# A four-layer AdaLN and FFN kernel on one core: small tiles and first-layer weights get other addresses in on-chip memory

## The reference

```python
# L0: 64x64 channel mix per sample, weights mixed by softmax(mlp(cond)); then top-1 routed LoRA (8 experts, rank 16)
out = einsum('boi,bih->boh', agg_w, x) + agg_b[:, :, None]
# L1, L2: grouped 9-tap convolution over the 1024 positions, plus a context vector per channel
out = conv(x, weight, groups=4) + ctx[:, :, None]
# L1 ffn: int8-style row-wise quantised product of 1024x1024
# L2 ffn: 1024x1024 base product + top-2 of 16 experts, rank 64
# L3: channel mix as L0; then up (1024x2048), relu^2, down (2048x1024), a latent path of 512
#     scaled by the two largest gate logits, and a layer norm with gamma, beta and LN_EPS
```

## Time and profile before

| | us |
|---|---|
| median of 3 runs | 1837.11 |
| lowest, highest | 1836.74, 1840.3 |
| the profiled execution's own time | 1837.11 |
| its span, first to last instruction | 1835.3 |
| PE busy | 1717.5 (94%) |
| DVE, ACT, POOL busy | 823.1, 459.5, 339.9 |

### The profile page before, as it was taken

The page is one execution under the profiler, slowest core; times in us unless marked ns, Lnnn a source line. Parts: engine busy times, 40 slices in busy tenths (PEclk is TensorE's granted clock), DMA queues, the critical chain, the costliest instruction groups (busy, mean ns, idle before and its releaser), DMA issues.

```text
span 1835.3 us, 22240 instructions
## 1 busy us (share of the span) xinstructions
PE 1717.5 (94%) x8396; PEld 1409.7 (77%) x8396; DVE 823.1 (45%) x1453; ACT 459.5 (25%) x694; POOL 339.9 (19%) x186
## 2 busy tenths in 40 slices
PE   7899837989889999999999999999999999999997
PEld 3578726878678888888768888888777888888876
DVE  4256579995534334433323333333272333333326
ACT  2344323433311111111122222221223222222212
POOL 1100011234223333333221111111201111111110
PEclk9999968999999999999999999999999999999999
DMA  8277414567633233323661111111192111111114
GB/s 311 93 185 187 134 43 139 165 202 233 213 110 94 96 107 119 94 95 108 174 195 46 47 58 56 46 46 46 66 358 75 52 46 46 46 46 46 46 58 161
DMA packets 126803, 205.80 MB, mean 112 GB/s; under 512 B 14436, under 2 KB 82092, under 8 KB 126124
## 3 DMA queue, kind: packets, MB, share of 16 engines
q1 hardware_dynamic: 109428, 154.21, 26.8%
q0 software_dynamic: 11264, 27.27, 4.6%
q10 hardware_dynamic: 6048, 23.46, 3.8%
HBM read 143.01 MB, written 61.89 MB: 112 GB/s over the span
## 4 chain that ended last, share of the span: by engine, by line
PE 72%; DVE 7%; DMA 5%; SPq 1%; issue 1%; ACT 1%; POOL 0%; DVEq 0%; ACTq 0%
PE pd L1414 24%; PE pu L1414 23%; PE l_po L1414 18%; PE pf L1414 2%; DMA scratch_x<-l_x 2%; PE l_py L1388 1%; PE l_pr L1372 1%; DVE row_peak L838 1%; DMA l_base_lo<-scratch_y_lo 1%; SPq L446 1%; DMA X<-scratch_x 1%; DMA scratch_y_lo<-y_out_lo 1%; PE l_pc L1338 1%; DVE y1T L863 1%; ACT row_mag L790 1%
## 5 line engine op out<-in xcount | busy, mean ns | idle before, releaser
L1414 PE MATMUL pd<-down_hi,hid_hi 128*128 128x512 f32 x640 | 249.1, 389 | 2.9 <-issue 2.9
L1414 PE MATMUL pu<-l_base_hi,up_hi 128*128 128x512 f32 x640 | 249.2, 389 | 0.0
L1414 PE MATMUL pu<-l_base_lo,up_hi 128*128 128x512 f32 x640 | 249.0, 389 | 0.0
L1414 PE MATMUL pd<-down_hi,hid_lo 128*128 128x512 f32 x640 | 249.0, 389 | 0.0
L1414 PE MATMUL pd<-down_lo,hid_hi 128*128 128x512 f32 x640 | 249.0, 389 | 0.0
L1414 PE MATMUL pu<-l_base_hi,up_lo 128*128 128x512 f32 x640 | 249.0, 389 | 0.0
L1537 POOL TENSOR_TENSOR down_lo<-raw,down_hi 128x1024 fp32r<-128x1024 f32 x40 | 100.3, 2508 | 701.1 <-ACT down_hi L1550 701.1
L1702 DVE TENSOR_TENSOR hid_lo<-hidden,hid_hi 128x512 fp32r<-128x512 f32 x64 | 44.8, 700 | 395.8 <-ACT hid_hi L1611 395.8
L1642 DVE TENSOR_TENSOR acc<-pd,acc 128x512 f32<-128x512 f32 x224 | 143.6, 685 | 54.8 <-PE pd L1414 51.5
L1605 ACT ACTIVATE hidden<-pu 128x512 f32<-128x512 f32 x64 | 38.3, 598 | 462.4 <-PE pu L1414 462.4
L1414 PEld LDWEIGHTS pd<-down_hi,hid_hi 128*128 128x128 f32 x640 | 120.1, 188 | 28.7 <-issue 3.7
(11 more groups left out here) (244 smaller groups left out, 2841.4 us busy)
## 6 DMA issues: line engine op xcount, KB each, us to landing
X<-scratch_x SPq DMA_DIRECT2D x256, 64.0 KB, 2.7
l_x<-scratch_x SPq DMA_DIRECT2D x32, 512.0 KB, 4.6
raw<-in_up SPq DMA_DIRECT2D x32, 512.0 KB, 3.6
raw<-in_down SPq DMA_DIRECT2D x32, 512.0 KB, 4.3
x_in<-in_x SPq DMA_DIRECT2D x16, 512.0 KB, 4.2
scratch_x<-x_in SPq DMA_DIRECT2D x16, 512.0 KB, 3.9
scratch_x<-l_x SPq DMA_DIRECT2D x16, 512.0 KB, 5.7
scratch_y2T<-y2T SPq DMA_DIRECT2D x16, 512.0 KB, 3.0
```

The costliest lines, as they stand in the source:

```text
L1414: mm = pe.matmul(out, lhs[a], rhs[b], start=first and n == 0, stop=last and n == len(pairs) - 1)
```

## The change

Only addresses change. Each engine of the changed program has the same instructions in the same order, with the same shapes, semaphores and waits, and each DMA moves the same bytes; the changed lines only shift line numbers by two or three further down.

```diff
-SMALL = D
+SMALL = D + NT * EG + 7 * NT
@@ l0_buffers
-    names["l0_wb"] = s_.sb("l0_wb", [P, D])
+    names["bias0"], names["sumA"] = s_.sb("bias0", [P, NT]), s_.sb("sumA", [P, P + E0])
+    names["l0_wa"], names["l0_wb"] = s_.sb("l0_wa", [P, KC, P + E0]), s_.sb("l0_wb", [P, D])
     names["taps0"] = [s_.sb(f"taps0{i}", [P, GROUPS, P]) for i in range(2)]
-    names["bias0"], names["sumA"] = s_.sb("bias0", [P, NT]), s_.sb("sumA", [P, P + E0])
-    s_.sb("l0_locals", [P, SMALL - NT - P - E0 + 4 * D + 3 * D])
-    names["l0_wa"] = s_.sb("l0_wa", [P, KC, P + E0])
@@ l3_buffers
     names["scratch"] = s_.sb("scratch", [P, D])
+    names["logits"], names["top"] = s_.sb("gate_logits", [P, NT // 2 * EG]), s_.sb("gate_top", [P, NT // 2, EG])
+    names["gate_sum"], names["sums"] = s_.sb("gate_sum", [P, NT]), s_.sb("row_sums", [P, NT, 2])
+    names["rows"] = [s_.sb(n, [P, NT]) for n in ("neg_mean", "sum_sq", "root", "rstd")]
     up1, raw1 = s_.split("up1", [P, D]), s_.sb("raw1", [P, D])
...
     names["act_f"], names["gamma"] = s_.sb("hidden", [P, 2, HALF]), s_.sb("gamma", [P, D])
-    names["logits"], names["top"] = s_.sb("gate_logits", [P, NT // 2 * EG]), s_.sb("gate_top", [P, NT // 2, EG])
-    names["gate_sum"], names["sums"] = s_.sb("gate_sum", [P, NT]), s_.sb("row_sums", [P, NT, 2])
-    names["rows"] = [s_.sb(n, [P, NT]) for n in ("neg_mean", "sum_sq", "root", "rstd")]
-    names["eps"] = s_.sb("eps", [P, 16])
@@ phase_l3
-    y, gate, eps = K["l2_base"], K["gate_s"], buf["eps"]
+    y, gate, eps = K["l2_base"], K["gate_s"], K["eps"]
@@ build
         K["low_loaded"] = s.slot_sems("low_loaded")
+        K["eps"] = s.sb("eps", [P, 16])
...
-                pool.memset(buf3["eps"][:], LN_EPS)
+                pool.memset(K["eps"][:], LN_EPS)
```

## The result

The changed kernel takes 1849.57 us against 1837.11 us, a ratio of 1.0067 (95% interval 1.0053 to 1.0082): 12 us slower, outside the range of the prediction (1834.0 to 1840.8). The profiled execution took 1848.27 us.

The account below looks back on a forecast made before the run. The prediction took PE, busy for 94%, to bound the kernel. With no work added and every address term taken as 0, the sum was 1837.1 + 0 = 1837.1 us, range 1834.0 to 1840.8 us.

Parts of the forecast that it names:

- Bounds: Whole kernel: PE busy for 94%, with 72% of the chain; L3 a string of 5.44 us pieces without waits.
- Layer-0 weights, small tiles, the 1024 bytes: cost 0: L0 operands, small tiles and tiles moved by 1024 bytes: 0; bounds 2.9 us either way for taps0 and l0_wb, 0.2 us for sumA.
- Tiles that gain 64 bytes: Tiles in L1, L2 and L3 going from remainder 192 to 0, such as down, hid and up0: claimed cost 0.
- For PE the same rows answer: L2 and L3 matmuls: L0's matmul rows include remainders 0 and 192 with one time to 3 ns, so 0.
- Rival B: L3's matmuls slower at their new addresses: 120 pieces x 0.04 = 4.8 us, time 1841.9 us; chance 0.06.
- its sign on that row: In L3's down product, pd<-down would show above 389 ns if matmuls paid for their operands' new places.
- DMAs: 0, and -0.4 us by a page: Exposed L0 stores and L2 input load: taken as 0, bounds -5.1 and +3.8 us; the skill's rule gives stores -0.4 us.
- Rival A: Exposed DMAs at new remainder 0, in L0's end and L2's load, fall to least landing: -5.1 us, 1832.0 us; chance 0.07.

Follow-up runs that it names:

- no64: The changed kernel without its 64 bytes in front: eps among the small tiles, the gap grown to 1024 bytes; 1836.22 us, ratio 0.9999.
- micro2: No kernel computation: strings of 96 matmuls on zeros behind 48 settling ones, plus narrower columns and plain float32; 21.76 us aligned, 22.40 us with weights at 64.
- micro: No kernel computation: PE alone runs strings of 24 split-form matmuls at varied weight and column addresses, then stores and loads; strings 5.44 to 5.63 us.
- all256: The changed kernel with eps ahead of y1T and l2_base, 64-byte gaps and layer-0 weights reordered, so every large tile starts at a multiple of 256; 1835.08 us, ratio 0.9991.
- before64: The kernel before with one gap of 64 bytes behind l2_base and nothing else; 1850.51 us, ratio 1.0075.
- up0back: The changed kernel with gaps that return, of the split-form tiles, only up0 to remainder 192; 1844.27 us, ratio 1.0048.
- micro3: No kernel computation: strings of 96 split-form matmuls on zeros in patterns of alternating or fixed weight and column remainders; 21.92 to 22.39 us.

## Why the prediction was wrong

- *Bounds.* Right: PE bounds L2 and L3, its pieces stand on the chain without a wait, and each nanosecond of them went into the time.
- *Layer-0 weights, small tiles, the 1024 bytes: cost 0.* Right, and shown by no64 to about 2 us, with the layer-0 weights at 32; at 96, in the changed kernel, `ph`, `po` and `pv` have the medians of before (279, 592 and 275 ns).
- *Tiles that gain 64 bytes, "For PE the same rows answer": cost 0.* This step failed. The earlier trace rows hold all differences in steps of 32, but of another form: plain float32, with two records a matmul, and 136 columns. The split form with 512 columns has the cost and was never in those rows; micro2 shows none at 256 columns and none in the plain form. In the up, down, base and expert products every operand lay at remainder 192, so the earlier trace rows held one case only, and what is seen in one case has no bound from it. But the kernel before did run one split-form product at other differences: L3's gate product, whose weights `gate_hi` and `gate_lo` start at 192 too and go on in chunks of 32 bytes, against `l2_base` at 192. Its 48 matmuls stood on the chain, and PE ran them at full clock:

```profile
1374.16 11.29 PE pd L1414 x48
```
```profile
1374.16 0.39 PE L1414 MATMUL pd<-l_base_hi,gate_hi 128*8 128x512 f32 x1 [1.92 <-DVE acc L1638]
...
1385.28 0.40 PE L1414 MATMUL pu<-l_base_hi,up_hi 128*128 128x512 f32 x1
```

From its first start to that of the next product are 11.12 us, 231.7 ns a matmul, where the pieces of 5.44 us have 226.7. An estimate from the steps of micro and micro2 for the eight differences 0 to 224 (one at 226.7, one at 229, six at 233.3) is 231.9 ns. These weights have 8 columns and not 128, so the row was a warning and no proof, but it is the row that the prediction needed: in place of 0, the bound would have been 5 ns a matmul, or 0.12 us a piece of 24.
- *Rival B.* It had the place and the side, with a chance of 0.06. Its price, 0.04 us a piece taken from L2's 5.48, was a quarter of the 0.16 us of `up0`, and it left out L2 (+4.7 us). Of its two groups the `up0` pieces paid 0.16 us and the `pd` pieces 0.02 to 0.04; `pd<-down` kept its median of 389 ns, so its sign on that row did not show. The 5.48 us of L2 is not this cost: it stays in all256.
- *DMAs: 0, and -0.4 us by a page.* No gain shown. The load of the L2 input took 7.59 us after 7.18. The last three waits for a store took 2.69, 2.66 and 3.00 us, 0.4 us less in all than before; but no64, with `x_in` at 192, has 2.90, 2.69 and 2.98 us, 0.2 us less. The Trainium skill, page "DMA: Bandwidth & Descriptors", section "How a descriptor splits into AXI transactions", says that the bytes in front of an unaligned start are fetched too and cost beats. By it, as an estimate, a store from remainder 0 is 4.5% shorter than one from 192. In micro it was 0.02 to 0.03 us of 2.6 shorter, about 1% of the time from issue to issue. The 3.2 us ahead of L2 come in other kernels without any alignment.
- *Rival A.* It fell with the time. What it is about, DMAs whose time goes by an address, does seem to show in L0 of before64 and all256, but with the windows `X`, which this change left at 192.

What is shown: the cost goes by the difference of the two start addresses, needs no other engine, and accounts for L2 and most of L3; about 2 us of L3 are `pd` pieces whose own operands lie alike, and go with their neighbours (up0back). That the two reads of PE meet in the memory is argued only; own and next pair could not be told apart. The Trainium skill says under "TensorE: Matmul & The Clock Gate", "Step-by-step: what each phase is for", that weights and moving columns have a read port each and that loading the next weights takes no bandwidth from the running matmul. In micro the time of a matmul was not free of how the two lie to each other: with PE alone at work, its step went from 226.7 to 233.3 ns by 64 bytes. Whether that is bandwidth, the runs do not show.

## What to carry to other kernels

Where PE bounds a stage of split-form float32 matmuls with 512 columns, place weights and moving tiles at the same remainder modulo 256 bytes, and products that alternate at one remainder for all; a 64-byte tile ahead of them cost 0.7% here. An edit of addresses alone is no empty edit. A row shows that something is free only for its own form of instruction, so look for a row with the form that bounds the stage, in its small products too (here the gate product), and where none varies what the edit varies, keep the range open.

## What the runs showed of the hardware

- A 128x512 split-form matmul follows the last after 226.7 ns where weights and columns start alike modulo 256 bytes, 232 to 234 ns where weights start 32 to 160 or 224 bytes further, 229 ns at 192, 226.7 ns at 240 (micro2). At 384 columns 48 matmuls took 8.34 us alike and 8.48 us at 64; at 256 columns the order is the other way by 2 ns a matmul; at 320 and for plain float32 there is none.
- What ran before counts: weights 16 bytes further were fast (5.45 us) behind a fast string and slow (5.60 us) behind a slow one (micro).
- Alternating remainders costs 0.48 us on 96 matmuls even where each pair lies alike (22.24 against 21.76 us, micro2 and micro3).
- Loads of 64 KB into windows at a multiple of 256 bytes landed in 2.3 us, at remainders 64 and 192 in 2.6 to 2.7 us, with the DMA engines less busy (0.53 and 0.52 against 0.59 to 0.62); the layer-0 weights moved with them.
